# Attention of a transformer block in even steps: a PSUM bank per head, row-tiled maxima, projections in thirds, spread row work, reciprocals by block transposes

## What is computed

```python
x = x + layernorm(attn(layernorm(x)));  x = x + layernorm(ffn(layernorm(x)))
kqv = xn @ Wqkv + bqkv            # 3 x 16 heads x 32; named q, k, v in this order
scores = einsum('bsnh,btnh->bnst', k, q) / sqrt(32)
scores = triu(scores) - 10000 * tril(ones, -1)
attn = softmax(scores, axis=2)
out = einsum('bnkq,bknh->bqnh', attn, v) @ Wo + bo
h = silu(xn @ Wg.T) * (xn @ Wu.T);  ffn = h @ Wd.T    # weights dequantised, inner width 2048
```

## Time and profile before

| | |
|---|---|
| median of three runs | 1863.56 us |
| the profiled execution's own time | 1863.75 us |
| its span, first to last instruction | 1862.0 us |
| granted TensorE clock over the span | 0.971 |
| before the first score | 114.9 us |
| 16 groups of attention | 1041.8 us |
| feed-forward and end | 705.3 us |

### The profile page before, as it was taken

The page is one execution under the profiler, slowest core; times in us unless marked ns, Lnnn a source line. Parts: engine busy times, 40 slices in busy tenths (PEclk is TensorE's granted clock), DMA queues, the critical chain, the costliest instruction groups (busy, mean ns, idle before and its releaser), DMA issues.

```text
span 1862.0 us, 25259 instructions
## 1 busy us (share of the span) xinstructions
PE 1719.7 (92%) x10015; PEld 782.5 (42%) x10016; DVE 1062.0 (57%) x1779; ACT 716.1 (38%) x1271; POOL 332.4 (18%) x558
## 2 busy tenths in 40 slices
PE   3889899998899989899989788999999999999997
PEld 1433333343333333233333223555555555555554
DVE  5545864685864686765695576724343333434254
ACT  3335555444555445555435454222222222222221
POOL 2212222133222223222222133100000000000000
PEclk7989999999999999899999989999999999999999
DMA  5111111122111222101222255311010100101000
GB/s 175 35 35 36 37 44 35 47 74 86 51 31 35 59 70 78 51 19 35 69 68 69 58 189 161 120 35 45 23 46 29 40 35 34 40 30 39 29 23 23
DMA packets 59174, 104.17 MB, mean 56 GB/s; under 512 B 11440, under 2 KB 11440, under 8 KB 59056
## 3 DMA queue, kind: packets, MB, share of 16 engines
q1 hardware_dynamic: 59056, 102.56, 18.3%
HBM read 51.92 MB, written 25.17 MB: 41 GB/s over the span
## 4 chain that ended last, share of the span: by engine, by line
PE 72%; DVE 16%; ACT 3%; issue 3%; DMA 2%; SPq 2%; POOL 1%; DVEq 0%; ACTq 0%; POOLq 0%
PE ps L669 24%; PE ps L686 13%; PE ps L578 8%; PE ps L634 6%; PE ps L644 6%; DVE mcol L872 5%; PE ps L601 4%; PE ps L620 4%; PE ps L589 4%; DVE st L779 2%; PE ps L655 2%; SPq L469 2%; DVE rec L900 2%; ACT pt L748 1%; PE ps L559 1%
## 5 line engine op out<-in xcount | busy, mean ns | idle before, releaser
L748 ACT ACTIVATE pt<-ps,nrm 128x512 f32<-128x512 f32 (+3 forms) x768 | 389.5, 584 | 363.7 <-PE ps L620 363.4
L669 PE MATMUL ps<-x2in,gu 128*128 128x512 f16 x2048 | 463.9, 380 | 0.0
L872 DVE TENSOR_REDUCE mcol<-ps 128x1 f32<-128x512 f32 (+3 forms) x608 | 357.4, 650 | 141.0 <-PE ps L604 128.4
L669 PEld LDWEIGHTS ps<-x2in,gu 128*128 128x128 f16 x2048 | 190.8, 98 | 244.4 <-issue 31.6
L601 PE MATMUL ps<-kpack,qpack 96*128 96x512 f16 (+3 forms) x768 | 218.3, 333 | 47.9 <-DVE yt L910 17.9
L944 DVE SCALAR_TENSOR_TENSOR hf<-ps,usc,sg 128x512 f32<-128x512 f32 x128 | 96.2, 751 | 270.0 <-PE ps L669 268.7
L686 PE MATMUL ps<-wd,hh 128*128 128x512 f32 x512 | 224.0, 438 | 0.0
L620 PE MATMUL ps<-qpack,kpack 98*128 98x512 f16 (+3 forms) x768 | 201.3, 335 | 18.5 <-DMA qpack<-mt 8.2
L686 PE MATMUL ps<-wd,hl 128*128 128x512 f32 x512 | 200.7, 392 | 0.0
L994 POOL TENSOR_SCALAR rs<-mv 128x1 f32<-128x1 f32 x128 | 26.3, 205 | 921.5 <-DVE mv L781 921.5
L634 PE MATMUL ps<-pt,v 128*32 128x512 f32 (+3 forms) x1536 | 172.4, 522 | 17.4 <-DVE atf L896 14.8
(11 more groups left out here) (103 smaller groups left out, 1622.8 us busy)
## 6 DMA issues: line engine op xcount, KB each, us to landing
qpack<-stage SPq DMA_DIRECT2D x192, 64.0 KB, 2.0
kpack<-stage SPq DMA_DIRECT2D x192, 64.0 KB, 2.0
xin<-in_x SPq DMA_DIRECT2D x32, 256.0 KB, 2.6
xr<-in_x SPq DMA_DIRECT2D x32, 256.0 KB, 2.9
x1d<-x SPq DMA_DIRECT2D x32, 256.0 KB, 3.2
x2d<-x2s SPq DMA_DIRECT2D x32, 256.0 KB, 2.0
x2in<-x2d SPq DMA_DIRECT2D x8, 1024.0 KB, 5.6
x1in<-x1d SPq DMA_DIRECT2D x8, 1024.0 KB, 5.7
```

Of the source, the lines that this page charges most:

```text
L669: mm = pe.matmul(bk, GU[:, c, m, i * 128:(i + 1) * 128], x2in[:, 1 - k, :, p, c, :], start=p == 0 and c == 0, stop=p == 1 and c == 3)
L748: act.activation(Pt[:, (step - 1) % 2, h, off:512], ps[:, BANK[job], off:512], ACT.Exp, scale=esc).then_inc(s_ex, 1)
L872: dve.tensor_reduce(mcol[:, n % 2, col:col + step * (nh - 1) + 1:step], ps[:, BANK[job], 0:nh * w].rearrange("p (h k) -> p h k", h=nh), AX ...
```

## The change

- **Banks.** Bank h (0 to 3) now belongs to head h: its maxima products and its scores share it in turn. Banks 4 and 5 take projections and transposes, 6 and 7 stay.
- **Maxima.** 12 lots for a group instead of 38 jobs: one query block for all four heads. Each head's product has 32 rows (the high halves alone, straight from `stage`, no longer from the DMA-made packs) and sits on its own 32 rows of the array (`tile_position`); the diagonal products follow for all four heads. DVE reduces the four banks one by one. Every step has one lot, of group n+1 (of n+2 in the last two).
- **A step** is now in this order: maxima lot, `den` of the step before, score of head 0, one third of a projection, scores of heads 1 to 3, `num` of the step before, more thirds, transposes, row work.
- **Projections in thirds**, by `woven` at two a step and more where needed; the drain of `qk` and `woproj` are jobs of their own (`qk_out`, `wo_out`).
- **Row work.** The eight chains of a sequence lie in its own g = 3 (three begin there), and in g = 0 and g = 1 of the next. The last sequence leaves five to the feed-forward part. `atT` has five slots, so that a new group doesn't overwrite it.
- **Reciprocals.** DVE transposes bank 7 in 32 x 32 blocks, takes the reciprocal of 16 columns instead of 512, and transposes back with a broadcast; one instruction then multiplies bank 6 by beta and by it. ACT's copy of bank 7 is gone.
- `ffn_load` goes over 20 steps of the last two groups instead of 8 and 12 steps with 12 loads each.

```diff
@@ -37,31 +37,91 @@
 
 def max_lots():
...
+    for qb in range(8):
+        if qb >= 4:
+            lots.append((qb, 0, 512))
+        first = qb // 4 * 512
+        lots.append((qb, first, (qb + 1) * 128 - first))
     return lots
 
...
+def rows_of(n):
+
+
+    b, g = divmod(n, 4)
+    out = []
+    chains = []
+    if g == 3:
+        chains = [(8 * b, (6, 7, 8, 9)), (8 * b + 1, (8, 9, 10, 11)), (8 * b + 2, (10, 11, 13, 14))]
+    elif g == 0 and b > 0:
+        chains = [(8 * b - 5, (1, 2, 3, 5)), (8 * b - 4, (3, 5, 6, 7)), (8 * b - 3, (6, 7, 8, 9)),
+                  (8 * b - 2, (8, 9, 10, 11))]
+    elif g == 1 and b > 0:
+        chains = [(8 * b - 1, (1, 2, 3, 5))]
+    for t, steps in chains:
...
         for s, (j, kb) in enumerate(STEPS):
-            for _ in range(2 if len(late) == 5 else 1):
-                if late:
-                    add(late.pop(0))
-            lots = [lot for p in plans for lot in p[s]]
-            cut = [lots[len(lots) * i // 4:len(lots) * (i + 1) // 4] for i in range(4)]
...
+                add(("mjob", of, lot))
+            over = pend is not None and pend[2] == 4 * pend[1] + 3
+            if pend is not None:
+                add(("den",) + pend)
+            if over:
+                add(("invert",) + pend[:2])
+            add(("score", n, j, kb, 0))
+            fill = list(slots[s])
+            if fill:
+                add(fill.pop(0))
+            for h in range(1, 4):
                 add(("score", n, j, kb, h))
-                for lot in cut[h]:
-                    plan.extend(lot)
             if pend is not None:
-                weigh(pend, cut[4])
-            else:
-                for lot in cut[4]:
-                    plan.extend(lot)
+                add(("num",) + pend)
+            plan += fill
+            plan += [("qk_out",) + job[1:] for job in slots[s] if job[0] == "qk"]
+            plan += [job for job in rows.get(12 * n + s, []) if job[0] == "wo_out"]
+            if s == 10 and n + 1 < NG:
+                plan += [("mjoin", n + 1), ("mturn", n + 1)]
+            plan += [job for job in rows.get(12 * n + s, []) if job[0] in ("ln1_turn", "turn2")]
+            if over:
+                add(("normalise",) + pend[:2])
+            plan += [job for job in rows.get(12 * n + s, []) if job[0] not in ("wo_out", "ln1_turn", "turn2")]
             pend = (n, j, kb)
...
@@ -208,25 +264,46 @@
...
+    elif kind == "mjob":
+        attention = True
+        for h in range(4):
+            take(("max",) + job[1:] + (h,), h)
+    elif kind == "score":
+        take(job, job[4])
...
+            k = 0 if closed[0] < closed[1] else 1
+            take(use, 4 + k)
+            closed[k] = len(PLAN) if kind == "part" else place
...
-                    at = 0
+                    e.wait_ge(s_qh, NO["qk", n, 0, qb // 4])
+                    e.wait_ge(s_qh, NO["qk", n, 1, (k0 + w - 1) // 512])
+                    for h in range(4):
+                        bk = bank(("max", n, i, h))
+                        rows = slice(32 * h, 32 * h + 32)
+                        mm = pe.matmul(bk[:, 0:w], stage[rows, 0, 0, qb * 128:(qb + 1) * 128],
+                                       stage[rows, 1, 0, k0:k0 + w], start=True, stop=not diag,
+                                       tile_position=(32 * h, 0))
+                        if not diag:
+                            mm.then_inc(s_mx, 1)
+                    if diag:
+                        for h in range(4):
+                            pe.matmul(ps[:, h, w - 128:w], low[:], id16[:], start=False, stop=True).then_inc(s_mx, 1)
...
@@ -626,35 +733,29 @@
...
                 elif kind == "den":
                     n, j, kb = a
                     ks = (STEP[a] - 1) % 2
                     off = max(0, kb - 4 * j) * 128
                     e.wait_ge(s_const, 7)
                     if kb == 0 and (n, j) != (0, 0):
-                        e.wait_ge(s_rc, 2 * n + j)
+                        e.wait_ge(s_dt, 2 * n + j)
+                    if kb >= 4 * j:
+                        e.wait_ge(s_dg, 8 * n + 4 * j + kb - 4 * j + 1)
                     for h in range(4):
+                        e.wait_ge(s_ex, NO["score", n, j, kb, h])
...
@@ -888,26 +981,27 @@
...
-                elif kind == "pull":
+                elif kind == "invert":
+                    n, j = a
+                    e.wait_ge(s_den, STEP[n, j, 4 * j + 3])
+                    dve.transpose(rec[:], DEN).then_inc(s_dt, 1)
+                    e.wait_ge(s_dt, NO[job])
+                    dve.reciprocal(inv[:], rec[:, 0:512:32]).then_inc(s_iv, 1)
+                    e.wait_ge(s_iv, NO[job])
+                    dve.transpose(rec[:], inv[:].unsqueeze(2).to_broadcast([128, 16, 32])).then_inc(s_rc, 1)
+                elif kind == "normalise":
...
-                elif kind == "normalise":
-                    n, j = a
-                    e.wait_ge(s_nm, NO[job])
-                    e.wait_ge(s_iv, 4 * NO[job])
...
+                    e.wait_ge(s_rc, NO[job])
+                    e.wait_ge(s_num, STEP[n, j, 4 * j + 3])
+                    dve.scalar_tensor_tensor(out=atf[:], in0=NUM, scalar=beta, in1=rec[:], op0=ALU.mult, op1=ALU.mult
+                                             ).then_inc(s_at, 1)
+                elif kind == "wo_out":
                     e.wait_ge(s_small, SCALED)
                     e.wait_ge(d_rows, 64)
                     e.wait_ge(s_wo, NO[job])
...
```

More of the change, by code:

```diff
@@ L51, in max_lots, with thirds, projections @@
     return lots
 LOTS = max_lots()
+LN1 = ("ln1_stats", "ln1_norm", "ln1_turn")
+WO_ = ("wo_out", "residual", "norm2", "turn2")
+def thirds(job):
+    return [("part", 0, job), ("part", 1, job), job]
+def projections(n):
+    b, g = divmod(n, 4)
+    due = []
+    if n + 2 < NG:
+        ends = ((4, 7, 10, 11), (3, 6, 7, 9), (2, 5, 8, 10), (2, 5, 9, 11))[g]
+        due += [(s, ("qk", n + 2, i % 2, i // 2)) for i, s in enumerate(ends)]
+    if n == 0:
+        due += [(s, ("vproj", 4 + i)) for i, s in enumerate((3, 5, 6, 7))]
+    if b + 1 < B:
+        ends = ((), (10, 11), (1, 4, 7, 11), (1, 4))[g]
+        first = 8 * b + 8 + (0, 0, 2, 6)[g]
+        due += [(s, ("vproj", first + i)) for i, s in enumerate(ends)]
+    return due
@@ new lines, in rows_of @@
+def rows_of(n):
+    b, g = divmod(n, 4)
+    out = []
[8 more added lines that the diff above has]
+    for t, steps in chains:
+        out += [(s, (kind, t)) for kind, s in zip(WO_, steps)]
+    if g == 1 and b + 1 < B:
+        for k in range(8):
+            out += [(5 + k + i, (kind, 8 * b + 8 + k)) for i, kind in enumerate(LN1)]
+    return out
@@ new lines, in woven @@
+def woven(due):
+    due = sorted(due, key=lambda d: d[0])
+    units = [(s, u) for s, job in due for u in thirds(job)]
+    room = [2] * 12
+    for more in (5, 7, 6, 8, 4, 9, 3, 2, 1, 0, 10, 11, 5, 7, 6):
+        left, at, slots, fits = list(room), 11, [[] for _ in range(12)], True
+        for s, u in reversed(units):
+            at = min(at, s)
+            while at >= 0 and left[at] == 0:
+                at -= 1
+            if at < 0:
+                fits = False
+                break
+            left[at] -= 1
+            slots[at].insert(0, u)
+        if fits:
+            return slots
+        room[more] += 1
+    raise ValueError("projections do not fit")
@@ L60, in order_of_jobs @@
     add = plan.append
-    ln1 = ("ln1_stats", "ln1_norm", "ln1_turn")
-    wo = ("woproj", "residual", "norm2", "turn2")
-    first = staged(ln1, list(range(8)))
+    first = staged(LN1, list(range(8)))
     add(("load_x", 0))
@@ L87, in order_of_jobs @@
     for i in range(len(LOTS)):
         add(("mjob", 0, i))
[L89 to L105, removed]
-            plan.extend(lot)
[L107 to L110, removed]
+        if fill and i % 3 != 2:
+            job = fill.pop(0)
+            plan += thirds(job)
+            if job[0] == "qk":
+                add(("qk_out",) + job[1:])
@@ L112, in order_of_jobs @@
+    plan += [("mjoin", 0), ("mturn", 0), ("packs", 1), ("mjob", 1, 0), ("mjob", 1, 1), ("ffn_scales",)]
+    rows = {}
+    for n in range(NG):
+        for s, job in rows_of(n):
+            rows.setdefault(12 * n + s, []).append(job)
+    pend = None
     for n in range(NG):
         b, g = divmod(n, 4)
[L114 to L118, removed]
@@ L195 @@
 for job in PLAN:
[L196 removed]
+    if job[0] in ("ln1_stats", "wo_out", "residual"):
         STAT[job] = len(STAT) + 1
```

276 lines of the change are left out of this document (128 added, 148 removed).

## The result

The changed kernel takes 1964.28 us (median of four runs, 1963.77 to 1964.78); beside it the kernel before took 1863.39 (four runs). The ratio is 1.0542, 95% interval 1.0523 to 1.0560: slower by 101 us. The forecast, 1902 in a range of 1835 to 1950, had the sign right and the size wrong. The profiled execution's span is 1962.3 us.

A forecast was written before the change was run, and what follows sets the result against it. PE was taken as the bound, with DVE's row work on top: a sequence takes 231 + 44 + 12.5 = 287.5 us against 275.4. Span 1862 + 36 (loop) + 1.6 (before first score) + 2 (feed-forward) = 1902 us, range 1835 to 1950.

The forecast's parts named there:

- Where the loss sits: In steps with transposes, PE's scores wait 2 to 3 us for DVE's reduce; g = 1 exceeds 64 us.
- 44 us of stalls: Per sequence, PE waits at score 0 for DVE's reduce behind row work, and similar waits: 44 us together.
- the step's own loop: In steps short of thirds, ACT's exponentials set the pace: about 3 us a group, 12.5 us a sequence.
- R2: Rival, 7%: PE's clock falls behind waits, to 0.95 in groups 1 to 12, giving 1925 us.
- the spread weight loads: Groups 13 to 15: loads over more steps should stop costing what they do there; clock 0.94 before.
- waits or a half clock: Kernel before: 31 of a sequence's 275 us, put down to 16 chains of row work, 1.9 us each.
- 231: PE's work for a sequence after the change, in us: 244 before, less 13 for the maxima.
- R3: Rival, 5%: the maxima's row tiles don't overlap; 12.1 instead of 6.3 us a group, giving 1960 us.
- 3.3 less a group: Maxima on PE by row tiles: 9.6 us a group becomes 6.3, 13 us less a sequence.
- R4: Rival, 2%: DVE's block transposes cost what the reciprocal does, 3.7 us instead of 0.7; over 2000 us.
- This buys nothing by itself: DVE's cheaper reciprocals save about 3 us twice a group, but DVE isn't the bound as a sum.
- R1: Rival, 31% faster, 5% level: waits no longer than now; 1830 us at half the waits, 1757 without them.

The follow-up runs named there:

- run 1: Changed kernel with residual, normalisation and statistics ahead of each step's transposes and their drains, no longer behind them: 1888.68 us, ratio 1.0139.
- run 2: Changed kernel with each step's transposes right behind score 3, ahead of `num` and the thirds; the row work stays at the step's end: 1859.55 us, ratio 0.9980.
- run 10: Changed kernel with only DVE's order altered: transposes' drains and row work stand behind the next step's four reduces: 1869.18 us, ratio 1.0031.
- Run 5: Changed kernel with 92 passes of zero-weight products added behind `den` in 57 steps where PE waits: 1950.41 us, ratio 1.0455.
- run 9: The kernel of run 8 with the maxima's products over all 128 rows in series, no row tiles: 1829.59 us, ratio 0.9818.
- run 6: Changed kernel with the maxima's products over all 128 rows in series, no row tiles: 1971.32 us, ratio 1.0567.
- run 7: Kernel before the change, with only the reciprocals done by two block transposes and one 16-column reciprocal: 1848.15 us, ratio 0.9914.
- run 8: Changed kernel with transposes and row work behind score 3, residual, normalisation and statistics ahead of the transposes: 1814.47 us, ratio 0.9726.

## Why the prediction was wrong

- **Where the loss sits: right.** PE's largest wait is L727 for L967, in the steps with transposes; g = 1 is longer than 64 us, 80.0; DVE is idle before L905 and L900, released by ACT. Runs 1, 2 and 10 cut the chain at three places, and each gives 76 to 105 us back.
- **The waits: right in size.** 44 us of stalls and 12.5 for the step's own loop were 56.5 a sequence; PE is idle for 53.5 in groups 4 to 7, 43.9 of them at score 0 and 37.2 of these right behind transposes. Single ones differ: 4.1 us in the worst step, once a sequence, where `residual` follows `turn2` and ACT's two drains come first (2.8 and 1.0 forecast), 1.4 to 2.5 in first-norm steps (1.9).
- **The failed step: the sum has no term for the clock.** It was put away as the rival R2, at 7%. R2's guess of the clock, 0.95 in groups 1 to 12, came true (the first row below). Its price was wrong: "a tenth of 850 us at half clock loses up to 42 us, half of it under the waits" put 1925, 23 us, where groups 1 to 12 alone lost 45.7 us. In the trace 121.1 of the 129.8 us at half clock fall on busy time, hardly any under the waits: the clock is down when work comes back, not while PE is idle. The loss is 60.6 us in place of 27.0, or 16.3 of the 19.6 us by which a sequence is over the forecast. Run 5 shows it by itself. R2 also had nothing for groups 13 to 15, where the forecast hoped that the spread weight loads would raise the clock: it fell from 0.93 to 0.91 (the second row), and 13.1 us were lost there.

```profile
179.40:1092.70 913.30, 755.98 (x5180) 256.08 (x5180) 513.63 (x1048) 397.76 (x720) 214.50 (x333) 0.95 0.17 48
1092.70:1254.80 162.10, 141.58 (x975) 42.14 (x976) 84.81 (x162) 81.31 (x155) 49.78 (x65) 0.91 0.40 121
```

  The mistake began with the reading of before: the 31 us of "waits or a half clock" were one number there, 19.8 idle and 3.3 clock in the trace of groups 4 to 7, with 8 us of work miscounted. I then priced waits, and no clock behind them.
- **The work: 6.3 us a sequence too low** (231, measured 237.3), as my count for before was 7.8 too low (244, measured 251.8). The difference of the two, which the change makes, is 14.5 and was forecast as 13: right.
- **The row tiles: right.** Each of the four starts 3 to 4 ns behind the one before, and a lot of 384 columns goes from 692.41 to 692.68 in the rows above. R3 is out. Their saving is real on PE, 43 to 49 us (runs 9 and 6; 16 x 3.3 = 53 forecast), but at most some 7 us of the time in this kernel and 15 in the best one. The "3.3 less a group" was taken for time; most of it was cover for the reduce.
- **The transposes: right.** Groups by line:

```profile
L991 DVE STREAM_TRANSPOSE rec<-inv 128x512 f32<-128x512 f32 x32 | 22.8, 711 | 1.1
L987 DVE STREAM_TRANSPOSE rec<-ps 128x512 f32<-128x512 f32 x32 | 22.6, 705 | 2.6 <-PE ps L756 2.6
```

  0.71 us, 0.7 forecast: R4 is out. "This buys nothing by itself" was wrong: it buys 18 us in the kernel before (run 7).
- **R1, faster, did not come, but its mechanism is the other side of the same price.** With the chains shortened by another order the kernel is faster, as R1 said it would be: run 8's 1814 lies between R1's 1830 and 1757.
- **R2, the clock, was no rival but a term.** The granted clock of the loop fell from 0.97 to 0.94. By that, the trace agrees with the Trainium skill (TensorE: Matmul & The Clock Gate, The HAM clock gate), which says that an idle PE loses its full clock. Not every wait costs it: of the 32 waits over 2 us in the loop, 24 have a spell at 1.2 GHz that begins from 1.2 us before to 2 us behind their end.

Waits and half clock are one case, and I had set them up as two. The forecast's 1902 with the measured 60.6 us of lost clock is 1963. That it fits so closely is partly luck: beside the clock, groups 4 to 11 are 6 us longer than forecast and the rest of the loop 7 us shorter. The range ended at 1950, since it took R2 by itself at 1925.

## What to carry to other kernels

Where an engine waits inside a loop, price two things: the wait, and the slower clock on the work behind it; in the kernels measured here, but one, the time lost at half clock was 0.2 to 0.35 of the idle time. Before a bank is shared between two uses, write down what stands ahead of the read-out in the queue of the engine that frees it, and put that queue's waiting work (a drain that hangs on another engine) last and its ready work first: the same jobs in another order were worth 150 us here. And work saved on an engine that waits is cover lost: 49 us of products saved were at most some 7 us of time here, and 43 us were 15 where the waits were short.

## What the runs showed of the hardware

- TensorE's half clock outlasts the wait: of 129.8 us at 1.2 GHz, 8.7 lay in idle time. Of the 30 spells at 1.2 GHz that begin in the loop, 28 begin from 1.1 us before to 1.8 us behind the end of a wait of PE over 0.9 us; of 75 such waits fewer than half were followed by one. Products with weights of zero are enough to keep it up: they raised the loop's clock from 0.94 to 0.97.
- Four products on their own 32 rows start 3 to 4 ns behind each other, and a full-width lot of them costs 0.32 to 0.33 us from its start to that of the next product, where four products of 128 rows cost 0.86 (run 9).
- DVE's float32 transpose in 32 x 32 blocks costs the same out of PSUM as from a source that is broadcast 32 times: 0.705 and 0.711 us for 128 x 512; the reciprocal of 16 columns, each 32 apart, takes 0.25 us.
- The first score came at 117.1 to 117.8 us in four kernels and at 119.4 to 121.3 in the six others that share its head but for small shifts. I did not find what sets it; up to 4 us of the differences between runs come from there.
